# A depthwise convolution's right tap on GpSimd, a copy moved to ScalarE, and all five engine lists re-ordered

## What is computed

```python
x = x + L0_xcond(layernorm(x), ctx, ctx, tau, delta)   # 16-head cross attention
x = x + L0_ffn(layernorm(x))                           # 8 bit linear, conv over time, silu, 8 bit linear
x = x + L1_xcond(ctx, layernorm(x), len, p_t)          # attention in a window of the context, tanh
x = x + L1_ffn(layernorm(x))                           # 8 experts, each token goes to one

# L0_ffn
h = bit_linear(x, w1)                  # 256 -> 1024
h = depthwise_conv1d(h, conv_w, conv_b)   # three taps over time: left, centre, right
h = silu(h)
return bit_linear(h, w2)               # 1024 -> 256
```

## Time and profile before

| | us |
|---|---|
| median of 3 runs | 449.95 (446.44 to 451.89) |
| profiled execution | 449.93 |
| its span, first to last instruction | 448.1 |
| TensorE busy | 345.9 (77%) |
| VectorE busy | 261.0 (58%) |
| ScalarE busy | 200.6 (45%) |
| GpSimd busy | 168.2 (38%) |

### The profile page before, as it was taken

The page is one execution under the profiler, slowest core; times in us unless marked ns, Lnnn a source line. Parts: engine busy times, 40 slices in busy tenths (PEclk is TensorE's granted clock), DMA queues, the critical chain, the costliest instruction groups (busy, mean ns, idle before and its releaser), DMA issues.

```text
span 448.1 us, 8255 instructions
## 1 busy us (share of the span) xinstructions
PE 345.9 (77%) x2713; PEld 265.1 (59%) x2713; DVE 261.0 (58%) x633; ACT 200.6 (45%) x535; POOL 168.2 (38%) x212
## 2 busy tenths in 40 slices
PE   6536589697998987987969678955361599999993
PEld 2423367475865756756748457642231588999982
DVE  3244544669898986986984885476417532222320
ACT  2401447586684973954845537414020134242320
POOL 3611403357283671761851514124130404242422
PEclk9565858999899998998997796575555599999999
DMA  6853460654715457176184030499530301111121
GB/s 196 294 138 70 107 163 15 149 130 106 164 38 127 105 148 208 40 203 162 25 222 102 1 117 1 150 393 352 191 121 1 95 0 46 48 47 59 31 61 36
DMA packets 36695, 52.24 MB, mean 117 GB/s; under 512 B 10495, under 2 KB 28744, under 8 KB 36390
## 3 DMA queue, kind: packets, MB, share of 16 engines
q1 hardware_dynamic: 28716, 34.78, 30.0%
q10 hardware_dynamic: 6288, 12.33, 8.4%
q0 software_dynamic: 1648, 4.59, 3.4%
HBM read 42.81 MB, written 9.31 MB: 116 GB/s over the span
## 4 chain that ended last, share of the span: by engine, by line
PE 54%; DVE 21%; DMA 10%; issue 6%; SPq 3%; POOL 2%; ACT 2%; DVEq 1%; POOLq 0%
PE ps L588 51%; DVE mx L1685 4%; DMA W<-nmT 4%; DVE W L1770 3%; PE ps L592 3%; DMA d_k<-W 2%; SPq L515 2%; DVE W L1571 2%; DVE hold L1571 1%; DVE W L1574 1%; DMA prepi<-in__lenS 1%; DMA d_q<-hold 1%; DMA out_x<-hold 1%; DVEq L1677 1%; DVE bst L1658 1%
## 5 line engine op out<-in xcount | busy, mean ns | idle before, releaser
L588 PE MATMUL ps<-W 125*32 125x112 f32 (+2 forms) x1280 | 96.4, 285 | 36.3 <-DMA W<-nmT 17.4
L588 PEld LDWEIGHTS ps<-W 125*32 125x32 f32 (+2 forms) x1280 | 70.6, 136 | 59.5 <-issue 23.8
L1685 DVE TENSOR_REDUCE mx<-ps 112x2 f32<-112x750 f32 x64 | 59.7, 934 | 38.5 <-PE ps L588 37.9
L1174 ACT ACTIVATE W<-ps 125x448 f32<-125x448 f32 x96 | 50.2, 542 | 33.6 <-PE ps L588 33.3
L588 PE MATMUL ps<-hold,proj 128*128 128x128 f32 (+2 forms) x288 | 57.3, 349 | 3.1 <-ACT W L1113 2.0
L588 PEld LDWEIGHTS ps<-hold,proj 128*128 128x128 f32 x288 | 40.7, 203 | 12.2 <-issue 4.6
L1346 ACT ACTIVATE hold<-ps,consts 128x128 f32<-128x128 f32 x88 | 25.2, 370 | 50.5 <-PE ps L588 50.5
L592 PE MATMUL ps<-consts,hold 112*128 112x112 f32 (+3 forms) x136 | 28.0, 302 | 21.6 <-DMA hold<-d_x,hold 5.6
L588 PE MATMUL ps<-hold 128*128 128x128 f32 (+4 forms) x256 | 38.0, 302 | 6.9 <-DVE hold L1571 5.2
L1459 POOL TENSOR_TENSOR rstd<-ve,expo 112x1 f32<-112x1 f32 x24 | 15.5, 648 | 71.8 <-DVE ve L1574 71.8
L588 PE MATMUL ps<-proj,hold 128*125 128x256 f32 (+1 forms) x128 | 40.8, 462 | 1.7 <-ACT hold L1088 1.0
(11 more groups left out here) (167 smaller groups left out, 546.8 us busy)
## 6 DMA issues: line engine op xcount, KB each, us to landing
W<-in_L_ffn_W SPq DMA_DIRECT2D x10, 1024.0 KB, 11.6
W<-in_L_ffn_W ACTq DMA_DIRECT2D x6, 1024.0 KB, 6.9
d_k<-W SPq DMA_DIRECT2D x16, 281.2 KB, 3.1
W<-d_k SPq DMA_DIRECT2D x16, 281.2 KB
hold<-in_ctxT SPq DMA_DIRECT2D x8, 375.0 KB, 3.7
W<-d_k SPq DMA_DIRECT2D x16, 187.5 KB
W<-d_q SPq DMA_DIRECT2D x48, 56.0 KB, 2.1
d_x<-hold ACTq DMA_DIRECT2D x8, 224.0 KB, 2.3
```

Of the source, the lines that this page charges most:

```text
L588: return pe.matmul(o, lhsT=l, rhs=r, start=start, stop=stop, skip_group_check=True)
L1174: act.activation(pexp[g % 2][0:LT, t, :], pE[n % 2][0:LT, 0:HG * T], ACT.Exp).then_inc(exp_done, 1)
L1685: dve.tensor_reduce(mx[:, 2 * i:2 * i + 2], pS[0:T, :, 0:L], X, ALU.max).then_inc(mx_done, 1)
```

## The change

Five things change. (1) The right tap and its sum go from DVE to POOL: `t_right` multiplies by the right tap into a new tile, `t_taps` adds it to the left tap, and `t_conv` of POOL, now last, counts `y_ready`. The four DVE instructions for each half go. The tile `right` lies over `hq`, so `t_right` waits for the previous batch's `t_down`. (2) `p_ew` is done by ACT. (3) PE's `t_h` of batch 0 waits for one cast of the weights and `t_down` for the other. (4) All five lists get a new order and new offsets. PE's new pass starts with the values and `a_scoresT(.., 0)`, has `t_dg2` behind that, puts more of `a_scoresT` ahead of `a_scores(.., 0)`, and has `p_q` and `u_wc` between `a_scores(.., 7)` and `a_max`. On DVE `t_silu(.., 1)` stands between `a_neg` and `a_nmT`, and `t_amax` behind it. On SP `a_stack` comes ahead of `p_qwrite` and `p_kread`. (5) In the ACT list `w_late` and `w_ffn` issue their loads earlier, and `w_early` runs two batches earlier, against the exponentials, than before (offset 7 against 5, where it was 12 against 8).

```diff
@@ -191,6 +191,7 @@
 hq = big[:, 3072:3072 + M0 * T // 2].bitcast(bf16).rearrange("p (m t) -> p m t", m=M0)
+right = big[:, 3072:3072 + M0 // 2 * T].rearrange("p (m t) -> p m t", t=T)
 stB = big[:, 1920:1920 + T]
@@ -556,21 +558,21 @@
     load_ctx(1)
-    for i in range(B + 4):
...
+    for i in range(B + 3):
+        w_delta(i - 1)
         p_rows(i)
...
+        a_stack(i - 2)
+        p_qwrite(i - 1)
+        p_ctx(i)
+        w_win(i)
+        p_kread(i - 1, 0)
+        p_qread(i - 1)
+        p_kwrite(i - 1, 1)
+        p_kread(i - 1, 1)
+        w_eb(i - 3)
+        w_tab(i)
+        p_ge(i)
+        p_kwrite(i, 0)
     sp.wait_ge(pv_ps, NG * B)
@@ -787,7 +789,7 @@
         if b == 0 and half == 0:
-            pe.wait_ge(quant, 2)
+            pe.wait_ge(quant, 1)
         pe.wait_ge(xqT_sb, b + 1)
@@ -816,6 +818,8 @@
     def t_down(b):
+        if b == 0:
+            pe.wait_ge(quant, 2)
         pe.wait_ge(hq_ready, b + 1)
@@ -878,56 +882,56 @@
     for i in range(B + 6):
...
         p_v(i - 1, 0)
         a_scoresT(i - 2, 0)
+        t_dg2(i - 4)
         a_scoresT(i - 2, 1)
...
         p_v(i - 1, 1)
         w_bo(i - 1)
+        a_scoresT(i - 2, 2)
         a_scoresT(i - 2, 3)
+        t_down(i - 4)
+        a_scoresT(i - 2, 4)
+        a_pv(i - 2, 0)
+        a_scoresT(i - 2, 5)
         t_xqT(i - 3)
...
+        a_scoresT(i - 2, 6)
         a_scores(i - 1, 0)
+        a_scoresT(i - 2, 7)
+        t_h(i - 3, 0)
+        a_scoresT(i - 2, 8)
+        w_sum(i - 1)
+        a_scores(i - 1, 1)
+        a_pv(i - 2, 1)
+        u_xn2T(i - 4)
+        t_h(i - 3, 1)
+        a_scores(i - 1, 2)
+        a_scoresT(i - 2, 9)
+        u_sc(i - 4)
         p_G(i - 2)
...
+        a_scores(i - 1, 3)
+        a_scoresT(i - 2, 10)
+        a_pv(i - 2, 2)
+        a_scoresT(i - 2, 11)
+        u_router(i - 6)
+        a_scores(i - 1, 4)
         p_k(i, 0)
...
+        a_pv(i - 2, 3)
+        a_scores(i - 1, 5)
+        u_alT(i - 4)
         p_k(i, 1)
...
+        a_scores(i - 1, 6)
+        t_oT(i - 2)
         p_x(i)
...
+        a_scores(i - 1, 7)
+        p_q(i)
+        u_wc(i - 4)
+        a_max(i - 1)
+        t_onT(i - 2)
+        p_V2(i - 2)
+        u_xn3T(i - 5)
+        t_oproj(i - 2)
+        t_amcT(i - 3)
     pe.wait_ge(filled, 1)
@@ -1139,6 +1143,17 @@
     @batch
+    def p_ew(b):
+        if b == 0:
+            act.wait_ge(s0_loaded, 16)
+        act.wait_ge(cxT_loaded[b % 2], 16 * (b // 2 + 1))
+        if b >= 2:
+            act.wait_ge(V2_ps, b - 1)
+        s0 = act.value_load(s0i[0:1, b:b + 1], min_val=0, max_val=L - WN)
+        copy(ew[b % 2][:, :, 0:WN], cxT[b % 2][:, :, bass.ds(s0, WN)]).then_inc(ew_made, 1)
+    @batch
     def p_cu(b):
@@ -1279,57 +1294,58 @@
         copy(cT[:, :, :], pZ[:, 0:DC * T].rearrange("p (k t) -> p k t", k=DC)).then_inc(xn3T_sb, 1)
-    for i in range(B + 12):
...
+    for i in range(B + 11):
+        u_alT(i - 8)
+        t_tanh(i - 7, 1)
+        p_q(i - 4)
+        p_qh(i - 4)
+        u_ln3(i - 9)
+        u_thx(i - 8)
+        w_late(i)
+        t_onT(i - 6)
+        p_qm(i - 4)
+        u_xn3T(i - 9)
+        p_V2(i - 6)
+        w_cast(i - 6, 0)
+        p_cu(i - 5)
+        p_kh(i - 4, 1)
+        p_v(i - 4, 0)
+        a_exp(i - 5, 0)
+        a_exp(i - 5, 1)
+        p_km(i - 4, 1)
+        p_v(i - 4, 1)
+        a_exp(i - 5, 2)
+        a_exp(i - 5, 3)
+        w_cast(i - 5, 1)
+        a_exp(i - 5, 4)
+        u_rows(i - 11)
+        a_exp(i - 5, 5)
+        t_xqT(i - 6)
+        a_exp(i - 5, 6)
+        w_early(i - 7)
+        a_exp(i - 5, 7)
+        u_ln(i - 7)
+        a_exp(i - 5, 8)
+        u_xn2T(i - 7)
+        t_center(i - 6, 0)
+        a_exp(i - 5, 9)
+        p_G(i - 5)
+        a_exp(i - 5, 10)
+        u_e(i - 7)
+        a_exp(i - 5, 11)
+        t_center(i - 6, 1)
+        p_kf(i - 3, 0)
+        t_osb(i - 5)
+        t_tanh(i - 6, 0)
+        p_kh(i - 3, 0)
+        w_ffn(i - 3)
+        w_gauss(i - 3)
+        p_ln(i - 3)
+        p_kf(i - 3, 1)
+        p_ew(i - 4)
+        p_x(i - 3)
+        p_km(i - 3, 0)
+        w_zero(i - 4)
     act.wait_ge(routed, LESS)
@@ -1443,12 +1459,32 @@
     @batch
+    def t_right(b, half):
+        pool.wait_ge(h_evac, 2 * b + half + 1)
+        if b >= 1:
+            pool.wait_ge(f_ps, b)
+        if half:
+            pool.wait_ge(taps_added, 2 * b + 1)
+        ms = slice(half * M0 // 2, (half + 1) * M0 // 2)
+        pool.tensor_tensor(right, hs[:, ms, 2:2 + T], cw[:, ms, 2:3].to_broadcast([128, M0 // 2, T]), ALU.mult)\
+            .then_inc(right_made, 1)
+    @batch
+    def t_taps(b, half):
+        pool.wait_ge(tap_made, 2 * b + half + 1)
+        pool.wait_ge(right_made, 2 * b + half + 1)
+        ms = slice(half * M0 // 2, (half + 1) * M0 // 2)
+        pool.tensor_tensor(th[:, ms, :], th[:, ms, :], right, ALU.add).then_inc(taps_added, 1)
+    @batch
     def t_conv(b, half):
         pool.wait_ge(yc_done, 2 * b + half + 1)
-        pool.wait_ge(tap_made, 2 * b + half + 1)
+        pool.wait_ge(taps_added, 2 * b + half + 1)
         ms = slice(half * M0 // 2, (half + 1) * M0 // 2)
-        pool.tensor_tensor(yc[:, ms, :], yc[:, ms, :], th[:, ms, :], ALU.add).then_inc(yl_done, 1)
+        pool.tensor_tensor(yc[:, ms, :], yc[:, ms, :], th[:, ms, :], ALU.add).then_inc(y_ready, 1)
     def ln_rstd(which, b):
@@ -1499,25 +1535,29 @@
         pool.tensor_tensor(xall[:, b, D:2 * D], x2[:, :], thx[:, :], ALU.add).then_inc(x3_ready, 1)
-    for i in range(B + 6):
...
+    for i in range(B + 5):
+        t_rs(i - 3)
         p_kr(i - 1, 1)
...
         p_kl(i - 1, 1)
...
+        u_rs3(i - 5)
         u_rs(i - 4)
...
+        p_cm(i - 1)
         t_tap(i - 3, 0)
+        t_right(i - 3, 0)
+        t_taps(i - 3, 0)
         t_conv(i - 3, 0)
+        t_tap(i - 3, 1)
+        w_eb(i - 2)
+        t_right(i - 3, 1)
         p_rs(i)
...
+        t_taps(i - 3, 1)
+        p_kr(i, 0)
         t_conv(i - 3, 1)
...
         p_x0b(i - 1)
         p_kl(i, 0)
+        p_qr(i)
+        u_x3(i - 4)
+        p_ql(i)
     pool.wait_ge(x0b_ready, B)
@@ -1666,17 +1706,6 @@
         ln_stats(x0[b % 2][:, :], 0, b)
-    @batch
-    def p_ew(b):
-        if b == 0:
-            dve.wait_ge(s0_loaded, 16)
-        dve.wait_ge(cxT_loaded[b % 2], 16 * (b // 2 + 1))
-        if b >= 2:
-            dve.wait_ge(V2_ps, b - 1)
-        s0 = dve.value_load(s0i[0:1, b:b + 1], min_val=0, max_val=L - WN)
-        dve.tensor_copy(ew[b % 2][:, :, 0:WN], cxT[b % 2][:, :, bass.ds(s0, WN)]).then_inc(ew_made, 1)
     @batch
@@ -1754,22 +1783,10 @@
             dve.wait_ge(yc_done, 2 * b)
-            dve.wait_ge(yl_done, 2 * b)
             dve.wait_ge(y_ready, 2 * b)
         m0 = half * M0 // 2
         tt(hs[:, m0:m0 + M0 // 2, 1:1 + T], pX[:, 0:M0 // 2 * T].rearrange("p (m t) -> p m t", t=T),
            stB[:, :].unsqueeze(1).to_broadcast([128, M0 // 2, T]), ALU.mult).then_inc(h_evac, 1)
-    @batch
-    def t_conv(b, half):
-        dve.wait_ge(h_evac, 2 * b + half + 1)
-        dve.wait_ge(yl_done, 2 * b + half + 1)
-        ms = range(half * M0 // 2, (half + 1) * M0 // 2)
-        for m in ms:
-            last = dve.scalar_tensor_tensor(yc[:, m, :], hs[:, m, 2:2 + T], cw[:, m, 2:3], yc[:, m, :],
-                                            ALU.mult, ALU.add)
-        last.then_inc(y_ready, 1)
     @batch
@@ -1862,46 +1879,43 @@
         tt(lgall[:, b, :], pZ[0:T, 0:NE], br_b[:, :], ALU.add).then_inc(lg_ready, 1)
-    for i in range(B + 18):
+    for i in range(B + 9):
         w_small(i)
...
+        t_silu(i - 7, 0)
+        a_max(i - 5, 6)
+        w_sum(i - 4)
+        t_norm(i - 6)
+        a_max(i - 5, 7)
+        a_neg(i - 5)
+        t_silu(i - 7, 1)
+        a_nmT(i - 5)
+        t_amax(i - 7)
+        u_stats3(i - 8)
+        t_x1(i - 6)
+        t_q2(i - 7)
         w_win(i)
...
+        t_hq(i - 7, 0)
+        w_quant(i - 5, 1)
+        w_quant(i - 5, 0)
+        w_bo(i - 4)
+        t_hq(i - 7, 1)
+        t_xq(i - 6)
+        t_x2(i - 7)
+        u_stats(i - 7)
+        a_max(i - 4, 0)
+        t_h(i - 6, 0)
+        w_scale(i - 4)
+        a_max(i - 4, 1)
+        p_stats(i - 3)
+        a_max(i - 4, 2)
+        w_delta(i - 3)
+        u_sc(i - 7)
+        a_max(i - 4, 3)
+        t_h(i - 6, 1)
+        a_max(i - 4, 4)
+        u_al(i - 7)
+        u_lg(i - 9)
+        a_max(i - 4, 5)
     dve.wait_ge(m_iota, 1)
```

More of the change, by code:

```diff
@@ L558, in _ @@
             load_ctx(1)
-            for i in range(B + 4):
[L560 to L570, removed]
-                p_rows(i)
-                p_kwrite(i - 1, 0)
-                w_delta(i - 1)
+            for i in range(B + 3):
+                w_delta(i - 1)
+                p_rows(i)
+                a_stack(i - 2)
[10 more added lines that the diff above has]
+                p_kwrite(i, 0)
             sp.wait_ge(pv_ps, NG * B)
@@ L905, in _ @@
[L905 to L911, removed]
-                u_sc(i - 4)
-                a_scoresT(i - 2, 6)
-                a_scores(i - 1, 2)
```

(67 more changed lines are left out.)

65 lines of the change are left out of this document (2 added, 63 removed).

## The result

The changed kernel takes 452.9 us (median of 20 runs, 449.2 to 457.0) against 449.6 for the kernel before on the same chips. The ratio is 1.007, with a 95% interval of 1.004 to 1.010: slightly slower, not 17 us faster. The profiled execution took 452.14 us with a span of 450.3 (before 449.93 and 448.1).

The account below looks back on a forecast made before the run. Order and waits, not one engine's load, bound the kernel: a loop through PE, DVE's maxima and their DMA. Won: periods 13.1, first two 1, start 4, less drain 1, so 17.1 off 449.93: 433 us, range 423 to 446.

Parts of the forecast that it names:

- The period of 28.0: Full pipeline periods, one batch each: 28.0 us, taken from loop routes by PE 27.6, DVE 25 and POOL 26.8.
- a rest case of 0.10: Slower or as before, through the second half or another wait in five re-ordered lists not walked to the end; chance 0.10.
- PE's 27.6: Loop route by PE: 18.6 us to the last scores, 2.6 queries and window product, 0.5 transpose and copy, 5.9 SP and DMA.
- The maxima's DMA: Transfer of negated maxima beside the queries, from nmT on: 5.9 us with SP, bounds 4.7 and 6.5.
- the rival of taking turns: POOL's added 4.2 us takes as much from DVE: periods win 5 instead of 13.1, time 441; chance 0.20.
- the sum's 21.2: DVE's work in a full period: 25.6 less 3.0 for the right tap and 1.4 for the context columns, 21.2 us.
- 1.06 us alone: DVE's four right-tap instructions of a half: 1.06 us alone, 2.00 while POOL computes; evidence for DVE and POOL taking turns.
- POOL's route: Loop by POOL: 6 us to the second layernorm's end, 13.5 of POOL work, 7.3 from tanh to DMA: 26.8.
- slower rival: Second half's sum too late when POOL's operations stretch by s: nothing won at 1.33, 2% slower at 1.57; within a 0.10 case.
- The first periods: First two periods, 57.2 us together, come down by 1; the third stays at 26.95.
- Start and drain: Up to the first cut 4 us won (5 won to 1 lost, perhaps 1 more); drain 1 lost (3 lost to 1 won).
- The tap's relief of 3 us: Right tap off DVE: 3.0 us a batch, both halves lying between maxima and hence in the loop.

Follow-up runs that it names:

- f1: Changed kernel with VectorE's first silu behind the negated maxima, context load behind the second keys' write, expert's load behind exponential 11: 427.1 us, 0.949 of the kernel before.
- g2: Changed kernel with VectorE's first silu behind the negated maxima and the expert's load behind exponential 11: 433.8 us, 0.968 of the kernel before.
- d4: Changed kernel with only the context's load behind the second keys' write and the expert's load behind exponential 11: 450.3 us, 1.002 of the kernel before.
- b1: Kernel before with only the right tap moved to GpSimd, all lists in old order: 454.2 us, 1.013 of the kernel before.
- a2: Changed kernel with the second half of the keys made and written earlier, ahead of the queries' read: 448.6 us, 0.998 of the kernel before.
- c1: a2 with the write of the keys' second half behind the queries' read again: 453.8 us, 1.012 of the kernel before.
- c2: c1 with VectorE's first silu moved behind the negated maxima: 448.0 us, four executions between 439.2 and 454.5.
- b2: Kernel before, old lists, with the right tap left out on every engine (result lacks that term): 436.2 us, 0.973 of the kernel before.

## Why the prediction was wrong

**The period of 28.0.** What failed is the step "I walk once round it ... three times: by PE, by DVE and by POOL", taken for the whole loop. Reads of keys and queries out of DRAM are routes of their own. I named the wait of `a_scores(.., 4)`, and the expert load in mid pass that could bring it about, only as signs of a miss, in a rest case of 0.10. Walked, the route is: cut to the read's issue 8.7 us, the read to its last landing 8 (184.06 to 192.08), 16.7 in all. PE was there 14.5 us behind the cut. The difference is the 2.2 us of wait. The other part of the 3.6 us lost in a period (31.4 against 27.8 in f1) is slower work: PE is busy 27.3 us with the matmuls that take it 25.4 in f1, where the clock stays full, and waits 0.4 less elsewhere.

**28 by another route.** g2 and f1 have 27.7 to 28.2 us in the full periods (the last 27.1 and 27.3), so the number was right for an undisturbed loop, but in part by luck. The longest of the three routes, PE's 27.6, held 5.9 us for the maxima's DMA; f1 has 3.7 from the end of `nmT` (186.11) to the cut (189.85), and PE does not wait there. What binds f1 is a chain that the prediction did not add up. Chain of waits in f1, from a cut on:

```profile
190.33 0.92 DVE W L1614
191.29 0.49 PE ps L590 x2
191.80 1.10 DVE W L1611
192.92 0.63 DVE W L1614
193.55 0.92 DVE hold L1614
```

It goes on over DVE to 198.8, over PE to 209.2, and over DVE's last maxima and negation to the next `nmT`.

**The maxima's DMA.** Taken at 5.9 us with 4.7 and 6.5 as bounds. In the kernel after, the cut at 206.85 comes 4.0 us behind the end of `nmT` at 202.83, and PE does not wait there, so the DMA took at most that: better than the lower bound. The argument, that the expert's load would no longer lie beside it, fits; I did not ask what the load would lie beside instead, and that was the read of the keys. The cost was moved, not removed.

**The tap on POOL and the rival of taking turns.** The rival was priced as a toll on every microsecond (DVE's route 29.2, in all 441). A toll of that kind did come, smaller than priced. DVE's busy time should have fallen to 21.8 (the sum's 21.2 took off 0.63 us of register load that was idle time, not work) and fell to 23.6. Two instructions behind the cut carry most of it, with 0.85 and 1.26 us of GpSimd's beside them; timelines of DVE and POOL after, where DVE took 0.27 and 0.41 before:

```profile
175.56 0.90 DVE L1614 TENSOR_SCALAR W<-consts,tiny 112x112 f32<-112x112 f32 x1
175.53 0.85 POOL L1409 TENSOR_TENSOR W<-W 128x375 f32<-128x375 f32 x1
178.69 0.99 DVE L1614 TENSOR_SCALAR hold<-hold,mv,rstd 112x256 f32<-112x256 f32 x1
178.28 1.26 POOL L1415 TENSOR_TENSOR W<-W 128x375 bf16<-128x375 f32 x1 [1.89 <-ACT W L1010]
```

f1 has the same two at 0.9 and 1.0, on the chain shown above. The large price comes in one place, at 2.8 to 4.6 us instead of 0.62, when a two-input instruction starts behind a gapless run on GpSimd. By the rule of the Trainium skill, "SBUF — State Buffer", section "Who interferes with whom", which the prediction weighed, whoever started first holds the pair; the rows of d4 and of the kernel after agree, and those of d4 show besides that a gapless run on GpSimd can keep VectorE's instruction out for three to five of its own. I had looked at the silu for lateness (none in the new lists) and not for length. The "1.06 us alone" for DVE's four tap instructions was misread too. POOL worked beside them, and it was POOL that took longer, 1.03 us for a scale step of 0.27; timeline of POOL before:

```profile
152.54 1.03 POOL L1460 TENSOR_SCALAR nmr<-mv,rstd 112x1 f32<-112x1 f32 x1
```

In the kernel after, POOL's three scale steps of a period take 1.4 us less, and its load is 19.4, not 20.9.

**POOL's route.** Forecast 6 + 13.5 + 7.3 = 26.8. In f1 the scale step starts 8.4 us behind the cut (170.28), not 6; POOL runs to the end of the second `t_conv` in 12.6 (182.86), and 7.0 follow to the next cut: 28.0, the length of the period, which is bound elsewhere. The slower rival's stretch s was 12.6 / 13.5 = 0.93, so this rival did not hold in the new lists; in the old ones (b1) it did.

**Queries.** The read of the queries is the next route: with the keys early (a2, c1, c2) PE came to `a_scores(.., 0)` up to 2.2 us ahead of it.

**The first periods.** Expected 1 us won, measured 7.1 lost; f1 has 82.7 us for the first three (before 84.2), so it was the same two causes: in the kernel after PE waited there 1.65 and 2.36 us for the queries' read, 2.19 behind a silu of 2.86 us (100.74) and 2.14 for the keys (129.59).

**Start and drain.** Start 4 us won was expected, 6.7 was measured: the queries' write is out of the chain, and the first scores start at 28.81 instead of 34.06. Drain 1 us lost was expected, 0.5 measured. Copy of the context columns: no wait behind it is seen.

**The tap's relief of 3 us** was right in size and in place, as b2 shows (13 us over the loop).

What stays open: why one wait of some 2 us is followed by many microseconds of the lower clock and another by few or none (see the last section). And c2's scatter of 15 us between executions isn't explained.

## What to carry to other kernels

Walk every route that closes the loop, with each read back from DRAM as one of them; a large load that is moved away from one small transfer must be followed to the small transfer that it meets next. When work is moved to GpSimd, look for the VectorE instructions that will start beside its longest gapless run, those with two SBUF inputs above all, and put them behind what other engines wait for. Two causes that hide each other look worthless one by one: here some 3 us each, hardly clear of the noise, and 26 together. And when a sum comes out, check that the chain of waits runs over the route that was summed.
